# A kernel whose five engines follow one sorted plan: every place in the plan is set anew, and a wait for the bias rows stands at two sequences

## The reference, cut to what matters

```python
for x in eight sequences:                                   # 256 x 128 each
    x = x + mamba(layernorm(x)); x = x + moe(layernorm(x))
    x = x + attend(layernorm(x)); x = x + moe(layernorm(x))

def mamba(x):
    hidden, gate = split(rmsnorm(x) @ in_w + in_b)          # 256 channels each
    h = silu(causal_conv4(hidden) + conv_b)
    ts, B, C = split(h @ xproj_w)                           # 64, 16 and 16 columns
    delta = softplus(ts @ dt_w + dt_b)
    for t in tokens:                                        # 16 states per channel
        state = exp(A * delta[t]) * state + delta[t] * B[t] * h[t]
        y[t] = (sum over states of state * C[t] + D * h[t]) * silu(gate[t])
    return y @ out_w + out_b

def moe(x):
    w = weights of the best 2 of softmax(x @ router_w), 0 elsewhere
    for e in 8 experts:                                     # 352 inner columns
        out = out + w[e] * ((x @ w_up[e] * silu(x @ w_gate[e])) @ w_down[e])
```

## Time and profile before

| | us |
|---|---|
| median of 3 runs | 628.21 (626.58 to 628.58) |
| span of the profiled execution, first to last instruction | 623.0 |
| median less span | 5.2 |
| PE busy, share of the span | 592.8, 95% |
| DVE, ACT, POOL busy | 499.4, 400.5, 392.6 |

### The profile page before, as it was taken

One profiled execution on the slowest core, in us unless ns is written; L12 is line 12 of the kernel. 1 busy time (PEld: TensorE's weight loads), 2 busy tenths in 40 slices (PEclk: granted clock), 3 DMA queues, 4 the chain that ended last, 5 costly groups with the idle time before them and its releaser, 6 DMA issues.

```text
span 623.0 us, 13130 instructions
## 1 busy us (share of the span) xinstructions
PE 592.8 (95%) x4502; PEld 546.7 (88%) x4502; DVE 499.4 (80%) x1094; ACT 400.5 (64%) x897; POOL 392.6 (63%) x368
## 2 busy tenths in 40 slices
PE   6778999699999999999999999999999999999997
PEld 5434786398989999999999999999999999999997
DVE  6798778886998799988998899889988896454454
ACT  7977727766768775878587867776576643516240
POOL 1486564589686987788787978697867773001000
PEclk9779999999999999999999999999999999999999
DMA  7952204130030403021302203030303000000000
GB/s 280 275 169 110 82 2 147 59 119 34 9 140 16 142 4 149 11 89 62 127 23 90 71 12 138 23 136 3 149 12 146 1 15 12 12 2 14 2 22 10
DMA packets 18468, 45.45 MB, mean 73 GB/s; under 512 B 2847, under 2 KB 13664, under 8 KB 14178
## 3 DMA queue, kind: packets, MB, share of 16 engines
q1 hardware_dynamic: 18402, 44.61, 20.1%
HBM read 40.15 MB, written 1.31 MB: 67 GB/s over the span
## 4 chain that ended last, share of the span: by engine, by line
PE 75%; POOL 6%; DVE 5%; issue 3%; ACT 2%; DVEq 0%; POOLq 0%; ACTq 0%
PE ps L1327 25%; PE ps L1131 13%; PE ps L1132 12%; PE ps L1133 12%; PE ps L1376 2%; POOL st L530 2%; DVE st L1005 2%; POOL yacc L543 2%; PE ps L1223 1%; PE ps L1388 1%; PE ps L1295 1%; DVE ps L991 1%; PE ps L1126 1%; PE ps L1367 1%; PE ps L1266 1%
## 5 line engine op out<-in xcount | busy, mean ns | idle before, releaser
L530 POOL TENSOR_TENSOR st<-st,rows_ring 128x512 f32<-128x512 f32 x128 | 165.7, 1298 | 58.5 <-DVE st L1005 58.2
L1327 PE MATMUL ps<-down,inner_ring 128*128 128x128 f32 (+1 forms) x1408 | 171.5, 274 | 0.0
L1327 PEld LDWEIGHTS ps<-down,inner_ring 128*128 128x128 f32 (+1 forms) x1408 | 165.5, 191 | 1.7 <-issue 1.0
L787 ACT ACTIVATE sg<-ps 128x512 f32<-128x512 f32 x176 | 104.3, 596 | 88.1 <-PE ps L1133 76.9
L1080 DVE TENSOR_TENSOR inner_ring<-sg,ps 128x512 f32<-128x512 f32 x176 | 118.7, 678 | 48.6 <-PE ps L1133 25.2
L1005 DVE TENSOR_TENSOR_SCAN st<-dA,ps 128x512 f32<-128x512 f32 x128 | 154.6, 1211 | 2.8 <-ACT dA L730 1.6
L543 POOL TENSOR_TENSOR yacc<-yacc,st 128x512 f32<-128x512 f32 x96 | 123.8, 1289 | 4.8
L730 ACT ACTIVATE dA<-delta,A 128x255 f32<-128x255 f32 x256 | 105.6, 494 | 3.1 <-POOL delta L522 2.8
L1131 PE MATMUL ps<-xhi,up_hi 128*128 128x256 f32 x352 | 104.5, 297 | 1.2 <-DVE inner_ring L1080 0.8
L1133 PE MATMUL ps<-xhi,up_lo 128*128 128x256 f32 x352 | 99.5, 283 | 0.0
L1132 PE MATMUL ps<-xlo,up_hi 128*128 128x256 f32 x352 | 99.4, 283 | 0.0
(11 more groups left out here) (160 smaller groups left out, 923.0 us busy)
## 6 DMA issues: line engine op xcount, KB each, us to landing
rows_ring<-bc SPq DMA_DIRECT2D x31, 1024.0 KB, 4.9
moved_rows<-inner_ring SPq DMA_DIRECT2D x96, 32.0 KB, 1.8
inner_ring<-gate_w SPq DMA_DIRECT2D x1, 1408.0 KB, 7.1
inner_ring<-up_w SPq DMA_DIRECT2D x1, 1408.0 KB, 9.7
down<-down_w SPq DMA_DIRECT2D x2, 512.0 KB, 10.7
out<-X SPq DMA_DIRECT2D x8, 128.0 KB, 1.8
rows_ring<-bc SPq DMA_DIRECT2D x1, 768.0 KB, 5.3
X<-x SPq DMA_DIRECT2D x1, 768.0 KB, 7.5
```

Source lines behind the costliest of these rows:

```text
L530: nc.gpsimd.tensor_tensor(st[:, i % NST], st[:, i % NST], row, ALU.mult).then_inc(s["m_p"], 1)
L787: nc.scalar.activation(sg[:, k % 2], two(bank_of(q, 2 * j)), ACT.Silu).then_inc(s["f_sg"], 1)
L1327: ins = nc.tensor.matmul(bank_of(q, 2 * NP + e)[:, c * H:(c + 1) * H], act_in, down[0:rows, e, n, :], start=n == 0, stop=n == NB - 1)
```

## The change

Every table of the plan gets new numbers. No operation is added, taken out or resized; the semaphores stand as they were, but for one: the wait for the bias rows.

```diff
-      "soft": -118.73, "early": -85.96, "early_step": 1.105, "late": -51.93, "late_step": 1.79, "scan": -77.19,
+      "soft": -118.587, "early": -84.716, "early_step": 0.981, "late": -51.499, "late_step": 1.895, "scan": -77.19,
...
-EXPERT = {"down": 1.13, "combine": 5.6}
+EXPERT = {"down": 1.107, "combine": 5.6}
...
-         "soft": [-6.4, 7.2, 3.5, 1.0], "early": [10.0, -8.7, -6.8, 0.1], "late": [-17.8, 8.6, 2.4, 0.0],
+         "soft": [-6.432, 7.079, 4.196, 1.087], "early": [9.677, -11.859, 0.894, -0.886], "late": [-21.82, -3.335,
+         3.456, -0.427], "attend": [0.392, -2.021, -1.575, -1.673, -1.344, -1.261, -1.86, 1.178]}
...
-           "split_up1": 93.33, "split_uv": 91.4, "load_x": 80.58, "load_down": 93, "lo_up0": 104.43,
-           "lo_up1": 113.81, "lo_uv": 160.34, "lo_up2": 118.86, "lo_up3": 123.42, "lo_rw": 100.12, "diag1": 65.9, "diag0": 74.1}
+           "split_up1": 107.139, "split_uv": 86.072, "load_x": 120.935, "load_down": 87.178, "lo_up0": 102.126,
+           "lo_up1": 108.518, "lo_uv": 189.931, "lo_up2": 114.277, "lo_up3": 123.387, "lo_rw": 104.139, "diag1":
+           66.91, "diag0": 73.821}
...
             def m_bias(u):
-                if u == 0:
+                if u < 2:
                     pool.wait_ge(s["d_bias"], 16)
```

More of the change, by code:

```diff
@@ L75 @@
[L75 to L83, removed]
@@ L111 @@
-LEAD = {"dbx": -7.25, "scan": -8.95}
-STATE = {"dbx": -2.07, "scan": -0.33, "mulC": 1.37, "sum": 4.4}
+AT = {"second": 34.732, "norm": -4.82, "norm2": -0.354, "route": 0.626, "pair": 1.656, "down": 19.472, "expert":
+      1.521, "attend_norm": 0.79, "attend": 9.468, "attend_stretch": 1.468, "in": -145.132, "in_stretch": 1.711,
+      "soft": -118.587, "early": -84.716, "early_step": 0.981, "late": -51.499, "late_step": 1.895, "scan": -77.19,
+      "state": 4.201, "rows": 14.458, "dx": -6.201, "y0": -23.937, "m_out": -2.404, "m_gate": 3.093, "weights":
+      -79.91}
@@ new lines @@
+PERIOD = 70.0
+M_IN = {"m_stats": -1.869, "m_pow": -1.435, "m_nb": 0.04, "m_norm": 1.605, "m_turn": 1.444, "m_hi": 2.896, "m_lo":
+        3.192, "m_ph": 4.341, "m_pad": 5.686, "m_tap0": 7.261, "m_cv": 6.326, "m_mul1": 5.808, "m_add1": 8.338,
+        "m_mul2": 8.527, "m_add2": 8.546, "m_mul3": 8.756, "m_add3": 8.967, "m_h": 11.467, "m_xp": 13.578, "m_xe":
+        16.997, "bc_out": 18.934, "m_dt": 16.448, "m_bias": 4.844}
+M_SOFT = {"m_abs": 7.486, "m_e": 9.699, "m_u": 10.519, "m_ln": 12.546, "m_v": 9.34, "m_pos": 12.976, "m_delta":
+          15.564}
@@ new lines @@
+SHIFT = {"m_stats": [65.425, -3.496, -3.12], "m_pow": [61.184, -9.616, -0.109], "m_nb": [63.366, -6.494, 5.181],
+         "m_norm": [60.901, -10.176, 3.518], "m_turn": [61.978, -8.576, 5.708], "m_hi": [61.665, -8.044, 4.022],
+         "m_lo": [63.161, -10.725, 3.706], "m_ph": [59.534, -10.117, 2.72], "m_pad": [59.595, -9.708, 1.033],
[3 rows of a table added]
+         [49.236, 5.853, 0.415], "m_xe": [45.065, 6.191, -4.938], "bc_out": [32.699, 5.738, 16.304], "m_dt": [46.931,
+         14.099, 1.343], "m_abs": [36.814, -7.123, -9.255], "m_e": [36.917, -4.462, -9.037], "m_u": [36.577, -3.52,
+         -3.527], "m_ln": [34.867, -2.005, 0.674], "m_v": [34.773, 2.884, 0.333], "m_pos": [34.382, 5.586, -0.327],
+         "m_delta": [32.642, 3.586, -4.878], "m_gate": [-7.909, 1.894, 2.614], "m_out": [-7.396, 3.113, 1.039],
+         "m_res": [-9.939, 0.173, 1.064], "m_dx": [0.698, -3.203, -1.711], "m_y0": [23.118, 5.243, 6.426], "m_pg":
+         [-14.916, 2.76, 0.182], "m_g": [35.343, 5.865, 3.761], "m_bias": [89.317, -2.698, 1.85]}
@@ L115, in start_of @@
+LEAD = {"dbx": -7.141, "scan": -7.028}
+STATE = {"dbx": -2.117, "scan": -0.31, "mulC": 0.703, "sum": 4.327}
 def start_of(s, which):
```

47 lines of the change are left out of this document (18 added, 29 removed), and 3 rows, old and new, of the table SHIFT.

## The result

The changed kernel takes 618.26 us (median of 4 runs, 616.19 to 618.30) against 627.39 us for the kernel before (4 runs): ratio 0.9864, 95% interval 0.9843 to 0.9886, both estimated from all the runs and not from the two medians. The direction is right, but the forecast has only about half of the size: it took 4.3 us off, the runs about 9. A later set of runs of both kernels (`changed_again`) gave 617.65 us and 0.9855 (0.9828 to 0.9881).

A forecast was written before the change was run, and what follows sets the result against it. The prediction took PE as the bound (busy 592.8 of 623.0 us), with gains only in the first 200 us. Terms -0.1 - 3.2 - 1.0 + 0 = -4.3 gave a 618.7 us span, plus 5.2 makes 623.9; range 621.3 to 628.0.

The forecast's parts named there:

- PE is full there: From 200 us to the end: PE works 417.4 of 423 us, so new orders win nothing; term 0, bounds -1.0 to +1.5.
- F1 to F3: 118 to 200 us: PE's 1.0 us wait for `h` goes as POOL makes it possible sooner; -1.0 us, bounds 0 to -1.5.
- the first stage: 0 to 58 us: the 2.38 us wait of `lo_rw` goes, but PE's list gives it back; -0.1 us.
- beside F0: 60 to 118 us: earlier decays and scans move sequence 1's gate from 118.19 to 115.0; -3.2 us, bounds 0 to -4.3.
- 5.2 us around the span: Whole kernel: 5.2 us lie between span and median, added to the forecast span of 618.7 us.
- a shorter L974: First stage: a shorter `m_dx(1)`, named with a clock staying high, for a bound of up to 1.5 us won.
- first stage keeps part: Rival, 0 to 58 us: part of `lo_rw`'s gain stays, through the clock or PE; -1.5 instead of -0.1, 622.5 us; chance 0.12.
- the first rival: End of sequence 1's layer: POOL's multiplies catch `m_dx(2)`, costing 1.8 us more; total -1.9, 626.3 us; chance 0.16.
- the fourth: Rival for 60 to 118 us: scans start sooner, but sums or banks hold the gate at 118; 627.1 us; chance 0.12.
- (b): 60 to 118 us: `m_xp(2)` goes first on PE, ending ACT's 6.07 us wait and scan 8's 1.60 us wait for its decay.
- (c): 60 to 118 us: DVE's scans no longer stand behind combines 0 to 2; scan 15 starts at 110.8, the gate at 115.0.
- The third rival: F3 to F12: `inner` behind a scan starves PE, 0.45 us a time; 9 us lost, about 632 us; chance 0.10.

The follow-up runs named there:

- s0_short_multiply: Kernel before, with POOL's multiply of state 15 of sequence 0 cut to 8 of each 256 columns: 0.9992 of the kernel before, first stage 37.0 us against 37.5.
- f3_all_new: Kernel before, with all five engines' new orders from F3 on: ratio 0.9973 to the kernel before, F3 to end 424.1 us against 425.9.
- f3_pe_new: Kernel before, with only PE's new order from F3 on: ratio 1.0040 to the kernel before, F3 to end 428.4 us against 425.9.
- f0_pe_old: Kernel before, with new orders up to F0 on all engines but PE: ratio 0.9969 to the kernel before, first stage 35.2 us against 37.5.

## Why the prediction was wrong, step by step

The step with the largest miss is "PE is full there": from F3 (194 us) on the forecast had 0, and the new orders won 1.8 us. Two further terms were too small: F1 to F3 (1.0 forecast, 2.5 measured) and the first stage, where `m_dx(1)` was left at its old length (0.1 forecast, 1.1 measured). The largest term, beside F0, held. The rest is the sum's 5.2 us around the span.

- **First stage, -0.1 (measured -1.1).** Right: the wait of `lo_rw` goes, `m_xp(1)` waits for `h`, the clock stays low until 42, the scan of state 10 starts where it did (0.3 us later). The sums, forecast to end at about 57, ended at 56.6. Wrong: `m_dx(1)`, which had stood for 2.51 us, was left in at its old length although POOL's work beside it moved too; it took 0.88. Before, the gate at 57.77 stood behind DVE's own steps and waited for nothing else, so this shortens its path by 1.6 us; PE's last sum then held it for 0.30. That the sums ended 0.6 us sooner, because PE's wait of 0.68 us for POOL at 47.94 was gone, let more through than the half microsecond of s0_short_multiply. The prediction named "a shorter L974" in its bound of -1.5, which held, but not in the term. The rival "first stage keeps part" had the right sign with the wrong reason given first (the clock).
- **Beside F0, -3.2 (measured -3.3).** In the old trace's time (57.77 - 56.64 = 1.13 us more than in the rows above), scan 11 was forecast at 100.7 and came at 101.0, scan 13 at 106.5 and came at 106.5, scan 15 at 110.8 and came at 110.8, the gate at 115.0 and came at 114.9. `m_dx(2)` took 0.67 us, so the first rival did not happen; nor did the fourth. What the text missed is that this is no sum of edits: the lists that carry (b), those of PE and ACT, cost 2.2 us alone, and the one that carries (c), DVE's, costs 4.5.
- **F1 to F3, -1.0 (measured -2.5).** This term was mis-sized. The wait for `h` went, by POOL's order, as reasoned (37.0 us from F1 to F2). But the earlier trace rows was one row of four. Of the other three rows of that view of the kernel before, shown below, the first two lie ahead of F3 and sum to 1.3 us (the wait for `xhi` is at 195 us, behind F3's start). I took half a microsecond of them as the far bound. In the changed kernel 0.5 us of waits are left instead of 2.3, and the stretch came out at -2.5, beyond the bound of -1.5. So the named waits are 1.8 of the 2.5; for the other 0.7 no view names a wait.

```profile
PE ps L1131 <- DVE inner_ring L1080: 0.8, 2, 0.6
PE ps L1223 <- POOL yacc L550: 0.5, 1, 0.5
PE ps L1295 <- ACT xhi L762: 0.2, 1, 0.2
```

- **From 200 us on, 0 (measured -1.8).** The step "PE is full there" led to no gain and a risk. From F3 on there were 2.0 us of waits in the view, 1.0 of them at two `m_pg` that the change moves; the experiment shows 0.6 from these two alone. f3_all_new shows that the orders behind F3 win the 1.8 us by themselves; by which steps the other 1.2 come stays open. The third rival, starved pairs, is refuted for the full set (0.2 us of waits for `inner` between F1 and F3, none behind). f3_pe_new shows that a new order can lose there too, but by waits for `n_xn` and `sg`, not for `inner`. (The rival's own sum gives 632.9, not about 632.)
- **Around the span, 5.2.** The forecast added the median of before less the span of its profile. The profiled execution of the changed kernel lasted 616.19 us with a span of 614.3, so 1.9 lies around a span. The fourth run of the kernel before, 624.87 us, is 1.9 above its profile's span of 623.0; the median of before stood 3.3 above that, because executions differ. In the result, median less span is 4.0, and 1.2 of the error of 5.6 us is this, 1.0 + 1.5 + 1.8 + 0.1 = 4.4 the terms.

## What to carry to other kernels

When all orders are set anew together, don't cost each moved step by itself: of the nine kernels that gave one stretch's new order to some engines and not to all, six were slower than before, one was 1.3 us faster in its stretch where the full set won 3.3, one 1.4 where the set won 2.5, and only f0_pe_old won more in its stretch than the full set. Where the bounding engine is 95% busy, don't call a stretch full and put it at nothing: here half of the gain (2.5 and 1.8 us) came in stretches whose waits were 0.2 to 1.0 us each. Adding up the rows of waits is the start of a bound and not the whole of it: the named waits fell by 2.1 us in stretches that won 4.3. And where two inputs of one step end nearly together, a saving on one gives only the distance to the other.
